# Six up products ahead of the first gelu, ScalarE's early list in another order, and expert output biases gathered by row instead of multiplied in

## What is computed

```
x = x + wkv(w, u, layernorm(x), ctx)        # a scan over time, one state per channel
x = x + ffn(layernorm(x))

gates   = softmax(xf @ gate_w + gate_b)      # 16 experts, the best 2 are kept
h       = gelu(xf @ ew1 + eb1)               # per expert, 128 hidden
eo      = h @ ew2 + eb2
routed  = sum over the 2 kept of gate * eo
hs      = gelu(xf @ sw1 + sb1)               # 2 shared experts, 2048 hidden each
shared  = hs @ sw2 + sum(sb2)
out     = shared + routed
```

## Time and profile before

| | us |
|---|---|
| median of 3 runs | 869.34 (869.12 to 870.53) |
| the profiled execution | 869.32 |
| its span | 867.7 |
| TensorE busy | 842.0 |
| VectorE busy | 598.4 |
| ScalarE busy | 471.7 |
| POOL busy | 192.4 |

### The profile page before, as it was taken

The page is one execution under the profiler, slowest core; times in us unless marked ns, Lnnn a source line. Parts: engine busy times, 40 slices in busy tenths (PEclk is TensorE's granted clock), DMA queues, the critical chain, the costliest instruction groups (busy, mean ns, idle before and its releaser), DMA issues.

```text
span 867.7 us, 14418 instructions
## 1 busy us (share of the span) xinstructions
PE 842.0 (97%) x4134; PEld 699.5 (81%) x4134; DVE 598.4 (69%) x1280; ACT 471.7 (54%) x843; POOL 192.4 (22%) x229
## 2 busy tenths in 40 slices
PE   3799999999999999999999999999999999999998
PEld 2567888888888888888888888888888889998886
DVE  8887898976677778556787786555687544443684
ACT  4687876454476554445556464345456356556441
POOL 4101000012100000112000002111121488754880
PEclk9999999999999999999999999999999999999999
DMA  8903644377352332584433324555697388868976
GB/s 217 291 30 97 159 133 134 98 153 145 83 164 89 100 107 85 115 199 86 146 111 98 96 86 96 122 101 169 178 230 179 104 255 283 262 212 272 321 220 217
DMA packets 127405, 135.45 MB, mean 156 GB/s; under 512 B 10520, under 2 KB 88912, under 8 KB 126828
## 3 DMA queue, kind: packets, MB, share of 16 engines
q1 hardware_dynamic: 117612, 108.47, 46.5%
q0 software_dynamic: 8784, 25.11, 9.7%
q10 hardware_dynamic: 944, 1.07, 0.4%
HBM read 111.63 MB, written 22.98 MB: 155 GB/s over the span
## 4 chain that ended last, share of the span: by engine, by line
PE 93%; ACT 0%; issue 0%; DVE 0%; ACTq 0%
PE up L638 13%; PE up L640 13%; PE up L639 13%; PE acc L704 13%; PE acc L701 13%; PE acc L699 13%; PE up L890 5%; PE acc L638 1%; PE acc L639 1%; PE acc L640 1%; PE misc L664 1%; PE up L664 1%; PE acc L815 1%; PE misc L723 1%; PE up L807 1%; PE misc L731 0%
## 5 line engine op out<-in xcount | busy, mean ns | idle before, releaser
L638 PE MATMUL up<-xs,w1hi 128*128 128x512 f32 (+1 forms) x512 | 199.0, 389 | 0.0
L640 PE MATMUL up<-xs,w1lo 128*128 128x512 f32 (+1 forms) x512 | 196.2, 383 | 0.0
L639 PE MATMUL up<-xs,w1hi 128*128 128x512 f32 (+1 forms) x512 | 195.7, 382 | 0.0
L699 PE MATMUL acc<-w2hi,hhi 128*128 128x512 f32 x486 | 189.9, 391 | 0.0
L701 PE MATMUL acc<-w2lo,hhi 128*128 128x512 f32 x486 | 189.6, 390 | 0.0
L968 ACT ACTIVATE hhi<-up,b_col 128x512 fp32r<-128x512 f32 x128 | 86.4, 675 | 155.0 <-PE up L640 130.6
L1253 DVE TENSOR_TENSOR hlo<-hf,hhi 128x512 fp32r<-128x512 f32 x128 | 85.7, 669 | 71.9 <-ACT hf L971 30.3
L704 PE MATMUL acc<-w2hi,hlo 128*128 128x512 f32 x486 | 131.0, 390 | 0.0
L638 PEld LDWEIGHTS up<-xs,w1hi 128*128 128x128 f32 x512 | 96.3, 188 | 18.8 <-issue 0.5
L640 PEld LDWEIGHTS up<-xs,w1lo 128*128 128x128 f32 x512 | 96.3, 188 | 18.9
L639 PEld LDWEIGHTS up<-xs,w1hi 128*128 128x128 f32 x512 | 96.5, 188 | 18.2
(11 more groups left out here) (283 smaller groups left out, 1081.1 us busy)
## 6 DMA issues: line engine op xcount, KB each, us to landing
w_raw<-in_L_ffn_sw SPq DMA_DIRECT2D x256, 256.0 KB, 3.1
expert_rows<-ysb SPq DMA_DIRECT2D x47, 256.0 KB, 3.4
xn_rows<-kn POOLq DMA_DIRECT2D x16, 256.0 KB, 7.5
e2raw<-in_L_ffn_ew SPq DMA_DIRECT2D x16, 256.0 KB, 5.1
ew_sb<-in_L_ffn_ew SPq DMA_DIRECT2D x16, 256.0 KB, 6.8
X<-in_x SPq DMA_DIRECT2D x12, 256.0 KB, 7.5
vin<-in_ctx SPq DMA_DIRECT2D x12, 256.0 KB, 11.2
out<-X SPq DMA_DIRECT2D x12, 256.0 KB, 5.1
```

The lines of the kernel that those rows point to most:

```text
L638: nc.tensor.matmul(o, lhs[0], rhs[0], start=start, stop=False)
L639: nc.tensor.matmul(o, lhs[0], rhs[1], start=False, stop=False)
L640: return nc.tensor.matmul(o, lhs[1], rhs[0], start=False, stop=stop)
L699: nc.tensor.matmul(acc[t][:], hh, w2hi[:, slot], start=first and (q > 0 or t >= HT) or again, stop=False)
```

## The change

The change has two parts.

In the early stretch six up products run ahead of the first down product instead of two. Products 3 to 5 use the second half of the banks of 0 to 2 (`up_piece`), and the first three gelus wait for their bank's second product. `RESULT_AT`, `X_AT` and the place of the fourth key transpose move accordingly. On ScalarE ek(1) moves behind the nine `grow` tables and two value copies, `x_full(1)` moves from before gelu 6 to behind the second reciprocal, and relu tables move.

In the bias part `cb96`, its transpose, `combine_T`, the loads and splits of `bias_r` and all bias matmuls go. For each tile POOL gathers, for both picked experts, the rows of `eb2` (`gather_bias`), and one tile later VectorE adds gate times row for both and the shared bias `bias_s` to `X2` (`route_bias`). The store of `rows_kept` moves behind the loop of weight loads and waits for these additions. The sum of the two shared biases is made once (`shared_bias`).

```diff
-        RESULT_AT = {2: 1, 8: 2, 14: 3}
-        X_AT = {4: 1, 10: 2, 16: 3}
+        RESULT_AT = {4: 1, 8: 2, 14: 3}
+        X_AT = {6: 1, 10: 2, 16: 3}
...
+        def up_piece(n):
+
+            at = n // RING if n < 2 * RING else 0
+            return slice(P * at, P * at + P)
...
-            sp.wait_ge(con.sem, con.at(0, "bias0"))
-            for r in range(3):
-                sp.dma_start(bias_f[32 * r:32 * r + E], eb2).then_inc(c_in, 16)
-                sp.dma_start(bias_f[32 * r + E:32 * r + E + S_EXP], sb2).then_inc(c_in, 16)
...
-                if q in (1, 2):
-                    sp.wait_ge(acc_free, TB * q)
-                    sp.dma_start(keep_dram[q - 1], X2[:, q - 1].rearrange("p t d -> p (t d)")).then_inc(keep_out, 16)
...
                     with sp.Fori(1, rounds) as i:
                         three(i)
+                if q in (1, 2):
+                    sp.wait_ge(acc_free, TB * q)
+                    sp.wait_ge(bias_ok, 3 * TB * q)
+                    sp.dma_start(keep_dram[q - 1], X2[:, q - 1].rearrange("p t d -> p (t d)")).then_inc(keep_out, 16)
...
-                    if isinstance(c, int) and n == CH - 1:
-
-                        pe.wait_ge(con.sem, con.at(0))
-                        pe.wait_ge(bias_hi, 3)
-                        pe.wait_ge(cbt_ok, TB * (q + 1))
-                        for t in range(TB):
-                            last = nc.tensor.matmul(acc[t][:], cbT[:, t], bias_r[:], start=False, stop=True)
-                        last.then_inc(acc_ready, 1)
...
-                pe.wait_ge(rt.sem, rt.at(t, "lo"))
-                nc.tensor.transpose(misc[0:BR, CBT0:CBT0 + P], cb96[:], ident[:])
+                pe.wait_ge(rt.sem, rt.at(t, "mem"))
...
-                need(pe, pre_h, n - 2)
+                if n >= 2 * RING:
+                    pe.wait_ge(pre_h, n - 2)
...
-            pre_up_product(1)
+            for n in range(1, 2 * RING):
+                pre_up_product(n)
             for n in range(N0):
-                if n == 2:
+                if n == 4:
                     key_T(3)
...
-                if n + 2 < N0:
+                if 2 * RING <= n + 2 < N0:
                     pre_up_product(n + 2)
...
-                act.wait_ge(pre_up, n + 1)
+                act.wait_ge(pre_up, n + 1 + RING if n < RING else n + 1)
...
-            early_exp(1)
             for b in range(CB // 2 - 1, CB):
                 table_grow(b)
             for i in range(HT, TB):
                 early_values(i)
+            early_exp(1)
...
-            x_full(1)
-            pre_gelu(6)
             pre_gelu(7)
             nc.scalar.preload_act_table_set("natural_log_exp_and_others")
             early_reciprocal(2)
+            x_full(1)
             early_exp(3)
...
-                    if j == 2:
-                        combine_T(TB * q + tb, tb, q)
...
+            def route_bias(q, t):
+                rows = X2[:].rearrange("p q t d -> p (q t) d")[:, t]
+                gate = c_all[:].rearrange("p n j -> p (n j)")
+                dve.wait_ge(bias_in, 32 * (t + 1))
+                need(dve, acc_free, TB * q)
+                for j in range(2):
+                    if j:
+                        dve.wait_ge(bias_ok, 3 * t + 1)
+                    V.scalar_tensor_tensor(out=rows, in0=bias_g[:, j], scalar=gate[:, bass.ds(2 * t + j, 1)], in1=rows,
+                                           op0=ALU.mult, op1=ALU.add).then_inc(bias_ok, 1)
+                after(con, 0, "shb")
+                dve.wait_ge(bias_ok, 3 * t + 2)
+                V.tensor_tensor(rows, rows, bias_s[:], ALU.add).then_inc(bias_ok, 1)
...
+            def gather_bias(t):
+                pool.wait_ge(rt.sem, rt.at(t, "bi"))
+                if isinstance(t, int) and t == 0:
+                    pool.wait_ge(con.sem, con.at(0, "shb"))
+                else:
+                    pool.wait_ge(bias_ok, 3 * t)
+                at = bias_at[:].rearrange("p n j -> p (n j)")
+                G.tensor_copy(bias_stage[:], at[:, bass.ds(2 * t, 2)]).then_inc(bst, 1)
+                pool.wait_ge(bst, t + 1)
+                apart(pool)
+                for j in range(2):
+                    pool.indirect_dma_start(out=bias_g[:, j], out_offset=None, in_=eb2[:, :],
+                                            in_offset=bass.IndirectOffsetOnAxis(ap=bias_stage[:, j:j + 1], axis=0))\
+                        .then_inc(bias_in, 16)
```

More of the change, by code:

```diff
@@ L181, in mixed_layer @@
         eb1_at = sb("eb1_at", [64, P])
-        bias_f = sb("bias_f", [BR, D])
-        bias_r = sb("bias_r", [BR, D], f32r)
-        lgT = bias_f[0:64]
+        lgT = sb("lgT", [64, D])
+        bias_g = sb("bias_g", [P, 2, D])
+        bias_at = sb("bias_at", [P, NT, 2], i32)
+        bias_stage = sb("bias_stage", [P, 2], i32)
         st6 = sb("st6", [P, TB, 6])
@@ L702, in __new__ @@
                     need(pe, h_lo, c + 1)
+                    ends = isinstance(c, int) and n == CH - 1
                     for t in tiles:
@@ L705, in __new__ @@
                                                 start=False,
-                                                stop=isinstance(c, int) and c == HOLD - 1 and acc[t] in y_bank)
+                                                stop=ends or isinstance(c, int) and c == HOLD - 1
+                                                and acc[t] in y_bank)
                     last.then_inc(down_done, 1)
@@ L935, in _ @@
                     nc.tensor.matmul(acc[t][:], hhi[:, slot, tok], w2lo[:, slot], start=False, stop=False)
[L936 to L937 removed]
+                    last = nc.tensor.matmul(acc[t][:], hlo[:, slot, tok], w2hi[:, slot], start=False,
+                                            stop=c == NCH - 1)
+                last.then_inc(tile_ready, 1)
         @block.scalar
@@ L1118, in _ @@
             early_reciprocal(1)
-            for n in range(3):
+            for n in range(5):
                 pre_gelu(n)
-            for n in range(3, 6):
+            for n in range(5, 7):
                 pre_gelu(n)
-                table_relu(n + 4)
-            x_full(1)
-            pre_gelu(6)
+                table_relu(n + 2)
             pre_gelu(7)
@@ L1136, in _ @@
             table_relu(11)
-            act.wait_ge(c_in, 16 * 10)
-            for at in (0, 32, 64):
-                nc.scalar.copy(bias_r[at:at + 32], bias_f[at:at + 32]).then_inc(bias_hi, 1)
-            for n in range(11, 13):
-                pre_gelu(n)
-                table_relu(n + 1)
+            pre_gelu(11)
+            table_relu(12)
+            pre_gelu(12)
             nc.scalar.preload_act_table_set("natural_log_exp_and_others")
@@ L1641, in _ @@
             const(V.memset(ones16[:], 1.0))
-            const(V.memset(cb96[:], 0.0))
-            after(con, 0, "cb0")
-            const(V.memset(cb96[:, E:E + S_EXP], 1.0))
-            const(V.memset(cb96[:, 32 + E:32 + E + S_EXP], 1.0))
             const(V.memset(f(gw2[:]), 0.0))
@@ L1655, in gate_weights, with shared_bias @@
                 const(V.tensor_tensor(gw2[:, :, 32:32 + E], gw_f[:], f(gw2[:, :, 0:E]), ALU.subtract))
-            def bias_low():
-                dve.wait_ge(bias_hi, 3)
-                const(V.tensor_tensor(bias_r[32:64], bias_f[32:64], f(bias_r[32:64]), ALU.subtract))
+            def shared_bias():
+                dve.wait_ge(s_in, 16 * S_EXP)
+                const(V.tensor_tensor(bias_s[:], bias_s[:], bias_g[:, 0], ALU.add))
             early_ln1(0)
```

79 lines of the change are left out of this document (33 added, 46 removed).

## The result

The changed kernel takes 861.93 us (median of 4 runs, 861.41 to 863.10), the kernel before on the same chip 869.36. The ratio is 0.9914, 95% interval 0.9902 to 0.9926: 7.5 us faster (6.4 to 8.5). 861.2 was predicted, in a range of 858.5 to 865.5. The profiled execution took 862.01 us with a span of 860.4, 7.3 less than before.

A forecast was written before the change was run, and what follows sets the result against it. TensorE, busy 842.0 of 867.7 us, was taken to bound the kernel. 869.32 less 3.76 (bias products), 1.76 (transposes) and 2.6 (early stretch) gave 861.2 us, range 858.5 to 865.5.

The forecast's parts named there:

- Term 1: Over the tiles and blocks: 16 bias products (3.76 us) and 16 transposes of `cb96` (1.76) taken off TensorE, 5.5 us.
- Term 2: Early stretch: ScalarE's new order brings the first shared up product to 66.1 from 68.74; gain 2.6 us, bounds 0.7 and 5.
- `b_col` at 21.2: Early stretch: with ek(1) behind tables and copies, ScalarE runs `b_col` at 21.2 instead of 24.60.
- the first up product at 24.5: Early stretch: TensorE starts it at 24.5 instead of 26.95, 2.1 us behind the transposes of `kn`.
- a wait of TensorE for `xf`: Early stretch, product 9: x_full(1) moves to about 44.2, the product wants it at 43.2; TensorE waits 1.7 us.
- result 2 set by VectorE: Early stretch: reciprocal(2) ends before VectorE's `num`, so TensorE takes result 2 at 47.8 instead of 49.74, 1.9 us ahead.
- Term 3: Tiles and blocks: added work of VectorE, POOL and the queues stays hidden; cost zero, VectorE +1.4 us a tile.
- the covers: Near 380: slack before TensorE needs `w2lo`, 5.8 us for its load and 5.0 us for VectorE's low weights.
- Rival A: Near 380: store and gathers delay the weight load past its cover, TensorE stops; 863.4, at most 865.3; chance 0.15.
- Rival C: In the tiles: gathers land late, VectorE stands, TensorE stops if they land after 15.1 us; 882 at 16.5; chance 0.05.
- Rival B: Early stretch: x_full(1) opens a gap longer than 1.7 us, or gelus come late behind product 3; 863.1; chance 0.17.
- Rival D: Early stretch: result 2 comes earlier and product 9's gap closes; gain 5 us, 858.8; chance 0.10.

The follow-up runs named there:

- The one moved line: The kernel before with only ScalarE's exponentials of key tile 1 (ek(1)) moved behind the last two value copies: 866.80 us, ratio 0.9970.

## Why the prediction was right, and where it was not

*Term 1* (5.5 us off TensorE): right in kind, 0.5 low in the profiled execution. By the times the bias part alone gives 5.2 (4.2 to 6.2). The blocks gave 1.60, 1.68, 1.67 and 1.07 us where I had 1.38 each. The bias products were priced well (0.94 us for four), the transposes at 0.11 when they cost 0.125, and 0.2 us a block stays open. The last 1.07, which holds the routed experts, varies: 1.65 in the kernel with the bias part alone, 0.92 in the repeat of the changed kernel.

*Term 2* (2.6 us): as a size of the gain from the early part right, 2.2 by the times (1.3 to 3.1). Its steps fared unevenly. Right: `b_col` at 21.2 (21.14), the first up product at 24.5 (24.13 to 24.73 in the traces), a wait of TensorE for `xf` (1.5 us at product 9, which wanted it at 44.5 and not at 43.2, 1.7 predicted; `xf` stands behind reciprocal(2), the third of the reciprocals, not the second as the description of the change has it), result 2 set by VectorE. Wrong: I gave gelu 0's wait for product 3 no cost. The table load stands behind that wait; preloading it took back 0.4 us. Wrong too: I gave TensorE's slow stretch one fixed length, that of before. It ended between 27.3 and 30.6 over the kernels with an early start, 2.9 to some 6 us after the first product, and differed by 2 us between kernels with the same early lists (3.8 and 5.9). The upper end of the forecast, 862.4, is the sum with 1.2 us for a slow stretch that ends where it ended before; no run shows that cost: with the early start full pace was there by 30.6 wherever products still ran to show it, and the loss that the table above has for the new order is 1.0 us, at 5.9 us of slow pace. In the profiled execution both errors met: product 5 ended at 33.57, the add for tile 1 came at 38.25 (before at 37.34), result 2 at 48.87 and not 47.8, result 3 at 61.21 and not 59.8, and term 2 was 1.24. In other traces of the same order it was 1.6 to 2.6. (The last parts of its sum, 59.8, 3.4 and 2.3, make 65.5 and not 66.1; from result 3 to the first shared up product the traces have 6.29 us before and after, which does give 66.1.)

And the reason that the term gave to its parts was off: I counted the gain to result 2, "1.9 us ahead", as the work of the new ScalarE order with six products as reserve. The one moved line alone brings result 2 to 47.24, 2.5 us ahead of before. The reserve is paid for with more than it brings: VectorE's add for tile 1 comes 3.4 us later than with the old order, and having reciprocal(2) in time gives back 1.7.

*Term 3* (0 us): right for the changed kernel. No stop near 380, and 1.6 us of waits for gathers (I had expected none), which TensorE does not see. VectorE's work rose by 19.4 us, 1.2 a tile, where I had 1.4. But the covers were thinner than I had them. The store near 356 landed in 10.1 us, where I had put 4.7, and ScalarE's wait doubled to 5.0. Of three kernels with the store in its place and the shared stage 1.6 to 2.1 us ahead of the changed kernel's, one lost 1.8 us there, one 0.6 and one nothing. *Rival A* is therefore real in the neighbourhood of this kernel, and its price is higher than I worked out, since a stop of 4.5 us cost a block 7.2: the other 2.7 us came at a granted clock of 0.63 and 0.52. I took 0 there because of a part of a landing time that the loads behind don't pay. The trace of before has it: the store at 236.50 took 4.9 us to land, and the weight load issued 1.3 us behind it 4.8, where one with no store ahead (285.37) took 2.7, so 2.1 of the 4.9 us were passed on. That the rest is fixed was not shown. *Rival C* is near too: gathers twice in series, with two more VectorE operations a tile, make 47 us.

*Rival B* happened in part: the profiled execution has 1.4 us less than term 2. Gelu 0 did come late behind product 3, but preloading the table took back only 0.4 of it. The rest, as an estimate: the first product came 0.2 late, the 5.9 us of slow pace, where before had 4.8, are some 0.5 by the table, and from result 2 to result 3 it took 12.3 us and not 12.0. *Rival D* did not; a closer relative of it, reciprocal(2) ahead of gelu 7, is worth 0.7 us.

The total came within 0.8 us because term 1 was 0.5 low and term 2, in that execution, 1.4 high. That the two errors had opposite signs was luck.

## What to carry to other kernels

When a change has several parts in one stretch, build each alone: here one moved line carried the whole early gain, and its more elaborate neighbour added only dependence on how long TensorE's slow stretch lasts. Here the gelu table's load stood behind its first user's wait (31.86, when ScalarE was free from 29.5); where a trace shows that, ask for it where the engine is idle. And where a large store is moved ahead of other loads on the same queue, measure in several traces how far the next consumer is from stopping: here ScalarE's wait differed by up to 4.6 us between kernels with the same store.

## What the runs showed of the hardware

At the start TensorE's matmuls of the early up products (128x128) stood 0.21 us apart, and later 0.11. The slow stretch, from the first of them on, is in the table above for ten traces. The other four are these (instants to within 0.2 us; the last column is TensorE's timeline from 27.0 on):

| kernel | first up | full pace | slow for | next up products |
|---|---|---|---|---|
| products in the order 0, 3, 1, 4, 2, 5 | 24.34 | 27.3 | 2.9 | 8 matmuls 1.24 us, the next 8 1.06 |
| reciprocal(2) ahead of gelu 7 | 24.30 | 29.2 | 4.9 | 16 matmuls 3.02 us |
| first store nine chunks later | 24.62 | 30.3 | 5.7 | 16 matmuls 3.39 us |
| gelu table ahead of the wait | 24.36 | 30.2 | 5.9 | 16 matmuls 3.46 us |

So it lasted 2.9 to some 6 us over fourteen traces. The window 20.00:40.00 has 1.00 in the granted clock column in each of the fourteen. The column does not show this pace, and the 1.00 of the earlier trace rows is no sign of full pace; the distances from start to start are. After a stop of 4.5 us in mid kernel the column does show a fall, to 0.52, and products of 512 columns stood 0.43 us apart for about 5 us.

Stores of 1 MB landed in 4.7 and 4.9 us before and in 10.1 and 11.3 after. The X loads behind the first are not what sets the two apart from those of before: the slower one, at 535.27, has none behind it. Both slow ones were issued within 1.5 us of GpSimd's scatters and its store of normed rows, which took 8 to 12 us to land there; the store moved to 447.97, with none of these beside it, landed in 6.5. That these are the reason was not tested.
